# The comparison loop of a sorted-attention kernel: q in three 16-bit parts, signs by pairs of heads, results two batches behind

## What is computed

```python
q, k, v = heads(x @ Wq + bq), heads(x @ Wk + bk), heads(x @ Wv + bv)   # 16 heads of 8
q_proj, k_proj = proj(q), proj(k)            # gelu MLP, (B, T, 16): one number per head
# both normed over T with a common deviation
Z = concat([k_proj, q_proj], axis=1)         # 2T numbers per batch and head
# sort Z; v and Z*v summed in that order (cumulative sums); each query takes its row
# out[q] = (Z_q * sum_{k <= q} v_k - sum_{k <= q} Z_k v_k) / (Z_q * count - sum Z_k)
```

## Time and profile before

| | |
|---|---|
| median of 3 runs | 1201.49 us (1201.22 to 1203.74) |
| profiled execution, first to last instruction | 1200.0 us |
| preparation | 109.3 to 130.9 us |
| loop of 16 batches, first spread to last result | 130.9 to 302.4 us |
| busy over the span | TensorE 73%, VectorE 64%, ScalarE 55%, GpSimd 43% |

### The profile page before, as it was taken

How to read it: one execution, slowest core, us unless ns; L and a number is a source line. 1 busy time by engine, 2 the same in 40 slices (tenths; PEclk the granted TensorE clock), 3 DMA queues, 4 the chain that set the end, 5 groups by cost and what they waited for, 6 DMA issues and landing times. The chain is left out here.

```text
span 1200.0 us, 20045 instructions
## 1 busy us (share of the span) xinstructions
PE 872.6 (73%) x5732; PEld 699.2 (58%) x5732; DVE 765.0 (64%) x2389; ACT 658.5 (55%) x1352; POOL 513.8 (43%) x634
## 2 busy tenths in 40 slices
PE   3796567675238999986995366777668989999910
PEld 2633455554227889975993133444457979999900
DVE  5479688887775457212676799998868641115636
ACT  4355777776635225653664676776775645555500
POOL 0002555555226666667774773000005663035155
PEclk9998777777557999997997688798867999999965
DMA  7960000000601126645763110000031133223132
GB/s 210 289 181 0 1 0 0 0 0 1 249 17 41 47 65 193 194 139 161 197 166 95 49 49 18 1 0 1 1 142 46 43 113 91 65 82 89 40 97 61
DMA packets 133845, 97.01 MB, mean 81 GB/s; under 512 B 11649, under 2 KB 125697, under 8 KB 132737
## 3 DMA queue, kind: packets, MB, share of 16 engines
q1 hardware_dynamic: 121472, 70.79, 19.7%
q0 software_dynamic: 12288, 25.19, 7.2%
HBM read 45.61 MB, written 50.33 MB: 80 GB/s over the span
## 5 line engine op out<-in xcount | busy, mean ns | idle before, releaser
L1122 POOL DMA_INDIRECT e_xs<-h_tok,rows_of x128 | 128.4, 1003 | 104.1 <-DVEq L1615 35.4
L735 ACT ACTIVATE mask<-ps_q,k_neg 128x256 bf16<-128x256 f32 x256 | 100.7, 488 | 34.8 <-PE ps_q L850 34.8
L1135 POOL DMA_INDIRECT e_got<-e_ys,e_rows_of x64 | 66.2, 1035 | 115.6 <-DMA e_ys<-e_y_rows 87.5
L850 PE MATMUL ps_q<-q_parts,pick 128*128 (+1 forms) x256 | 59.2, 367 | 50.0 <-DVE mask L651 41.6
L1778 DVE TENSOR_TENSOR e_hidden<-e_ps_gu,e_hidden 128x512 f32<-128x512 f32 x48 | 33.2, 691 | 96.8 <-ACT e_hidden L1461 96.6
L1271 PE MATMUL e_ps_gu<-e_w_all,e_x_turned 128*128 x384 | 92.0, 383 | 0.1
L1466 ACT ACTIVATE e_hidden<-e_ps_up 128x512 f32<-128x512 f32 x80 | 47.8, 597 | 73.4 <-PE e_ps_up L1309 73.2
L1122 POOL DMA_INDIRECT e_xs<-h_tok,e_rows_of x64 | 66.3, 1035 | 49.7 <-DVEq L1615 19.8
L1326 PE MATMUL e_ps_y<-e_w_all,e_h_turned 128*128 x640 | 84.2, 275 | 0.0
L2283 POOL DMA_INDIRECT c_got<-e_ys,rows_of x64 | 69.8, 1090 | 30.3 <-issue 19.2
L651 DVE TENSOR_TENSOR mask<-ps_q,k_tok 128x1024 bf16<-128x1024 f32 x64 | 75.1, 1214 | 9.2 <-PE ps_q L850 7.2
(11 more groups left out here) (410 smaller groups left out, 2597.4 us busy)
## 6 DMA issues: line engine op xcount, KB each, us to landing
e_x_rows<-e_xs SPq DMA_DIRECT2D x68, 256.0 KB, 2.9
e_ys<-e_y_rows SPq DMA_DIRECT2D x68, 256.0 KB, 2.4
e_xs<-zeros SPq DMA_DIRECT2D x2, 6144.0 KB, 34.2
e_w_all<-in_w SPq DMA_DIRECT2D x4, 1536.0 KB, 13.0
e_xs<-zeros SPq DMA_DIRECT2D x2, 2560.0 KB, 27.5
e_w_all<-in_w SPq DMA_DIRECT2D x4, 1024.0 KB, 11.0
x_tok<-in_x SPq DMA_DIRECT2D x4, 512.0 KB, 6.0
e_xs<-h_tok,rows_of POOLq DMA_INDIRECT x128, 2.3
```

Of the source, the lines that this page charges most:

```text
L735: last = nc.scalar.activation(mask[u][QS // 2 + j][keys][:, h * T:(h + 1) * T], psq[1][:, h * T:(h + 1) * T], ACT.Sign, bias=k_neg[u][:, k ...
L850: last = nc.tensor.matmul(psq[0 if on_dve else 1][:, h * T:(h + 1) * T], pick[:, (quad * HQ + h) * P:(quad * HQ + h + 1) * P], q_parts[:, ...
L1122: nc.gpsimd.indirect_dma_start(out=xs[part], out_offset=bass.IndirectOffsetOnAxis(ap=rows_of[:, t * K + k:t * K + k + 1], axis=0), in_=til ...
L1135: nc.gpsimd.indirect_dma_start(out=got[t % GB][:, k * P:(k + 1) * P], out_offset=None, in_=ys[part], in_offset=bass.IndirectOffsetOnAxis(a ...
```

## The change

1. `q_parts` and `pick` become bf16. q is held in three 16-bit parts, in rows 0 to 63, 64 to 95 and 96 to 127. `w2` therefore writes 128 columns (`PR` = 128), loaded in three DMA pairs instead of two. ScalarE's clearing of `q_parts` goes, and GpSimd's clearing of `qn` and `kn`.
2. Preparation is written out for all 16 batches and staggered. ScalarE rounds 128 rows at once, VectorE subtracts (rows 64 to 127), ScalarE rounds that (rows 64 to 127), VectorE subtracts again (rows 96 to 127). GpSimd takes no part.
3. ScalarE's quads are spread and read by pairs of heads, one bank each. `signs` takes both key tiles of two heads instead of four heads of one key tile. A bank is refilled as soon as its pair is read.
4. VectorE's `results` and GpSimd's `numerators` run two batches behind; VectorE's `sums_in` stands behind both masks. The total of the ScalarE quads is taken before the second VectorE spread.
5. Four more semaphores are made at the start.

The core of the diff:

```diff
-        PR = 2 * HR
+        PR = P
-        q_parts = sb("q_parts", N, F32R)
-        pick = sb("pick", HEADS * P, F32R)
+        q_parts = sb("q_parts", N, BF16)
+        pick = sb("pick", HEADS * P, BF16)
...
-                    nc.scalar.activation(q_parts[PR:P, :].rearrange("p (t c) -> p t c", c=P),
-                                         env["zeros"][PR:P, :].unsqueeze(1).broadcast_to([P - PR, TILES, P]),
-                                         ACT.Copy).then_inc(rows_cleared, 1)
...
+                    def without_high(b_):
+                        dve.wait_ge(high_out, FROM + b_ + 1)
+                        nc.vector.tensor_tensor(q_rest[u][LOW, :], qn[u][LOW, :], at(q_parts, b_ * T, T)[LOW, :],
+                                                ALU.subtract).then_inc(rest_out, 1)
+                    def last_part(b_):
+                        dve.wait_ge(mid_out, FROM + b_ + 1)
+                        low = at(q_parts, b_ * T, T)[LAST, :]
+                        nc.vector.tensor_tensor(low, q_rest[b_ % AHEAD][LAST, :], low, ALU.subtract).then_inc(parted, 1)
+                    for n in range(NB + 3):
+                        if n < NB:
+                            rows_normed(n)
+                        if 0 <= n - 1 < NB:
+                            without_high(n - 1)
+                        if n >= 3:
+                            last_part(n - 3)
...
                         if now:
                             masks(b_, parity, 0)
-                        if before:
-                            sums_in(b_ - 1)
+                        if is_at(b_, 0):
+                            constant_parts()
+                        elif not is_at(b_, 1):
+                            results(b_ - 2)
                         if now:
                             masks(b_, parity, 1)
-                        if before:
-                            results(b_ - 1)
-                        else:
-                            constant_parts()
-                    pipelined(dve, NB, step)
+                        if not is_at(b_, 0) and not is_at(b_, NB + 1):
+                            sums_in(b_ - 1)
+                    two_behind(dve, NB, step)
...
+                    def spread_for_dve(b_, quad):
+                        pe.wait_ge(masks_dve, FROM + b_ * (QS // 2) + quad)
+                        spread_heads(b_, quad, range(HQ)).then_inc(q_ps_dve, 1)
+                    def spread_for_act(b_, quad, pair):
+                        nth = (quad - QS // 2) * NP2 + pair
+                        if quad == QS // 2:
+                            pe.wait_ge(masks_act, FROM + b_ * (TPB * NP2) + (0 if is_at(b_, 0) else pair - NP2 + 1))
+                        else:
+                            pe.wait_ge(masks_act, FROM + b_ * (TPB * NP2) + nth - NP2 + 1)
+                        spread_heads(b_, quad, range(2 * pair, 2 * pair + 2)).then_inc(q_ps_act, 1)
...
                         if now:
-                            spread_q(b_, 0)
+                            spread_for_dve(b_, 0)
+                            for pair in range(NP2):
+                                spread_for_act(b_, 2, pair)
                         if before:
                             mask_values(b_ - 1, 1 - parity, 0)
                             mask_values(b_ - 1, 1 - parity, 1)
+                            signs_total(b_ - 1, 1 - parity)
                         if now:
-                            spread_q(b_, 2)
+                            spread_for_dve(b_, 1)
+                            spread_for_act(b_, 3, 0)
                         if before:
                             mask_values(b_ - 1, 1 - parity, 2)
                             mask_values(b_ - 1, 1 - parity, 3)
                         if now:
-                            spread_q(b_, 1)
-                            spread_q(b_, 3)
+                            spread_for_act(b_, 3, 1)
```

More of the change, by code:

```diff
@@ L62, in pipelined, with two_behind @@
     step(n, 0)
+def two_behind(eng, n, step):
+    assert n % 2 == 0
+    step(0, 0)
+    step(1, 1)
+    with eng.Fori(1, n // 2) as i2:
+        step(i2 * 2, 0)
+        step(i2 * 2 + 1, 1)
+    step(n, 0)
+    step(n + 1, 1)
 def is_at(i, n):
@@ L437, in _ @@
                 def _(act):
-                    for rows, first in ((slice(0, HR), 0), (slice(HR, PR), HR), (slice(PR, P), 0)):
+                    for rows in (slice(0, P // 2), slice(P // 2, P // 2 + HR), slice(P // 2 + HR, P)):
+                        first = rows.start
                         nc.scalar.activation(pick[rows, :].rearrange("p (h t) -> p h t", t=P),
@@ L587, in attention0 @@
             qn, kn = ([tb(f"{n}{u}", T) for u in range(AHEAD)] for n in ("qn", "kn"))
-            hi_r = [tb(f"hi_r{u}", T, F32R, rows=PR) for u in range(AHEAD)]
+            q_rest = [tb(f"q_rest{u}", T) for u in range(AHEAD)]
             cols = tb("cols", HEADS * VC)
@@ L625, in _ @@
                     env["inverse_root"](c, rs[:, :], pvar["k"][:, :], ptmp[:, 0:NB])
[L626 to L634 removed]
+                    LOW, LAST = slice(P // 2, P), slice(P // 2 + HR, P)
@@ L801, in step @@
                     def step(b_, parity):
-                        now, before = not is_at(b_, NB), not is_at(b_, 0)
+                        now = not is_at(b_, NB) and not is_at(b_, NB + 1)
                         if now:
-                            pool.wait_ge(qk_sb, FROM + AHEAD + b_ + 1)
+                            pool.wait_ge(qk_sb, FROM + b_ + 1)
                             parts = [vals[parity][:, j * HEADS * HV:(j + 1) * HEADS * HV].rearrange(
@@ L808, in step @@
                             remainder(b_ * TPB, parts[0])
+                        if not is_at(b_, 0) and not is_at(b_, 1):
+                            numerators(b_ - 2)
+                        if now:
                             third_part(b_ * TPB, parts[0])
@@ L862, in mask_values @@
                         if quad == QS // 2:
[L863 to L869 removed]
+                            pe.wait_ge(masks_act, FROM + (b_ + 1) * (TPB * NP2))
                         for h in range(HQ):
```

148 lines of the change are left out of this document (69 added, 79 removed).

## The result

The changed kernel takes 1184.6 us (median of four runs, 1183.8 to 1185.7) against 1201.6 us before (1201.2 to 1203.7): ratio 0.985, interval 0.984 to 0.987. The prediction was 1181.5 us with a range of 1177.0 to 1190.5. The profiled execution after has a span of 1183.9 us.

The account below looks back on a forecast made before the run. The prediction took a ring of waits between VectorE and TensorE, not one engine, to bound the loop. Loop -19.0, preparation +0.4 and first stage -1.4 sum to -20.0, giving 1181.5 us, range 1177 to 1190.5.

Parts of the forecast that it names:

- Loop, -19.0: Loop from first spread to last result: 8.95 us a batch, bounds 8.8 and 9.4, so 19.0 us gained.
- the gap of the loop's turn: VectorE in the loop: 0.33 us of "issue" idleness every second batch, counted in its 8.8 to 9.1 us.
- Both ends: First and last loop steps, replayed with the same durations: masks 1 of batch 1 end at 15.9 us, the loop at 153.4.
- TensorE's clock: Loop: shorter pauses could grant TensorE more clock, but would not move the sum, as VectorE's 8.9 us has no matmul.
- My rings of 8.75 and 8.8 us: Loop wait cycles at TensorE's slow rate: ScalarE to ScalarE 8.75 us, VectorE's sums to masks 1 8.8 us a batch.
- Preparation, +0.4: First norming to first spread: VectorE becomes the bound at four times 0.33 us a batch; +0.4 us, bounds -1 and +3.
- the signs that I had named for being wrong: Profile after: sums still waiting, results waiting for `num`, a batch over 9.4 us, or first spread later than 134 us.
- The clearing's term: First stage: without ScalarE's clearing of 3.60 us the projection ends near 21.85; -1.4 us, bounds -1.5 and 0.
- bf16 spreads: TensorE in the loop: 0 to 0.6 us less a batch, counted as nothing because TensorE is not the bound.
- TensorE's rings: Rival in the loop, chance 0.14: cycles through TensorE bind at its slow rate, 9.5 us a batch, total 1189.
- the rounding chain: Rival in preparation, chance 0.03: VectorE and ScalarE wait for each other, 2.9 us a batch instead of 1.3, total 1207.
- The rival of late numerators: Rival in the loop, chance 0.10: VectorE waits for GpSimd's numerators, 0.5 us a batch, total 1188.

Follow-up runs that it names:

- c1: Changed kernel with TensorE's spreads for ScalarE's first four heads moved behind two mask values and the signs' total of the batch before: loop 169.48 us, ratio 0.998.
- b4: Changed kernel with ScalarE's scratch refilled by whole groups of four heads, signs key by key: loop 196.81 us, ratio 1.024.
- c2: Changed kernel with VectorE's results one batch behind and GpSimd's numerators ahead of its last third part: loop 199.52 us, ratio 1.019.
- a4: Changed kernel with all waits of VectorE's preparation moved to the head of each turn: preparation 30.07 us, ratio 0.977.
- b3: Changed kernel with VectorE's sums back between the two masks, plus two added waits for the numerators: loop 176.05 us, ratio 1.008.

## Why the prediction was right, and where not

- **Loop, -19.0 against -23.2.** The mechanism was right: sums without a wait, VectorE's own work as the bound. The term mis-sized was the batch, 8.95 against 8.57 in the rows shown and 8.63 on average: I kept the gap of the loop's turn and results of 2.21. The turn now follows four queued sums of 0.5 us each and shows no gap; results take 2.00. Fourteen batches at 0.32 are 4.4 us, the whole difference. Both ends came as replayed: masks 1 of batch 1 end 16.0 us after the first spread (15.9), and the rest behind masks 1 of batch 15 takes 11.4 (12.2, less the 0.9 for a fast TensorE).
- **TensorE's clock.** I had said that a higher clock would not move the sum. The granted clock over the loop rose from 0.73 to 0.83 and was 1.00 in the batch shown. My rings of 8.75 and 8.8 us were worked out at the slow rate and are longer than the measured batch. Had TensorE stayed at that rate they might have bound; no run shows it, but that the clock could not move the sum did not follow from my own rings.
- **Preparation, +0.4 against +6.8, outside my bound of +3.** The first spread at 134.74 is one of the signs that I had named for being wrong (later than 134 us), and it holds for this stage. VectorE became the bound as said. Two things were mis-sized. I took the step of the norming (0.33) for all four instructions; `y_tok`, the row that I had named, gives a length of 0.43, and with the change of rows the step is the length and 0.03. Three such steps and one of 0.33 are 1.67. The norming took 23.9 us, where I had 19.1. And I followed only q's chain from its end to the first spread (2.9 us; it was 4.5): the key columns, their sums at TensorE's slow rate (2.08 us) and ScalarE's copy are the longer chain. This is 4.8 + 1.6.
- **Before the first norming, -1.4 against -3.0.** The clearing's term was near: the first projection starts at 22.30 instead of 23.22, the gelu stage 1.2 us earlier. (These 1.2 us are no larger than the scatter of the first norming.) The wide `w2` that I counted at 0 to +1.7 gained 1.6 to 1.7. I had compared the lengths of two weight loads and not read when they start.
- **bf16 spreads, 0.** Right within the scatter in the new loop. In the old one the same change goes with 7.9 us.
- **Four semaphores and two more DMAs, 0 to 0.2.** Nothing of them shows in the stages.
- **Behind the loop, 0 against +3.3** in the profiled executions and about +1 to +2.4 by medians. By medians the total is 3.1 us later than predicted: 2.4 come from here and 0.6 from the stages before. The stages add up to -19.4 where I had -20.0, by errors of opposite sign (-4.2, +6.4, -1.6): that is luck.
- **The range.** Its lower end does not follow from the terms that I named: -21 - 1 - 1.4 from 1201.5 is 1178.1, not 1177.
- **The rivals.** TensorE's rings did not bind and the rounding chain overlapped. The rival of late numerators had the right mechanism for the wrong kernel: in the changed kernel the results wait for them three times, 3.5 us in all, while in c1, b4 and c2 VectorE waits for them in all 16 turns (24.7, 45.5 and 29.5 us).

## What to carry to other kernels

When a loop is held by rings of waits through four engines, the order in which each engine's queue holds its work is one design: undoing one part of it lost about as much as the whole had gained, or more, and gains of two edits that remove the same wait do not add. A row gives the length of an instruction; the step to the next is shorter only where the rows of the trace show an overlap, so ask what differs (here, by all rows seen, the start rows) before you use the shorter one. And follow each chain to the end of a stage, keys as well as queries.

## What the runs showed of the hardware that I had not expected

- On VectorE, the preparation's instructions of 0.41 us that start at the same row follow each other every 0.33 us; where the start row changes, the next starts 0.03 us after the end (steps of 0.43 to 0.46, and 0.32 behind one of 0.29), with waits on them (after) and without (a4). A change in the number of rows alone did not stop the overlap (0.61 us from 128 rows and 0.69 us to one row, both from row 0).
- On TensorE, a weight load of 64 columns behind matmuls with 128-column weights was not taken ahead: the weight path idled for 0.76 us before it, against 0.24 for one of 128 columns. It cost 0.3 us in most groups of four tiles.
- The 0.33 us of a hardware loop's turn on VectorE are gone where the turn follows the queued sums (after), and come back as 0.20 to 0.21 where it follows results (b3, c2).
